# Gate logits in two halves, at steps 29 and 31, and the choice, gates and dispatch two steps later

## What is computed

```python
    x = x + _L0_conv_ref(_gn(x), ...)              # a scale per image and channel
    t = _to_tokens(x)                              # 1024 tokens of 128 per image
    t = t + _L1_attn_ref(_ln_t(t), ...)            # 8 heads of 16, softmax and a fixed decay
    t = t + _L1_ffn_ref(_ln_t(t), ...)             # 8 experts, the best 2 of each token
    x = _from_tokens(t, x)
```

```python
        logits = xf @ wg + bg
        top_vals, top_idx = jax.lax.top_k(logits, TOP_K)
        gate_w = jax.nn.softmax(top_vals, axis=-1)
```

## Time and profile before

| what | value |
|---|---|
| median of three runs | 2371.93 us |
| the profiled execution, its own time | 2371.68 us |
| its span, first to last instruction | 2369.9 us |
| PE busy, share of the span | 2076.4 us, 88% |
| DVE busy | 1897.7 us, 80% |
| ACT busy | 1460.3 us, 62% |
| POOL busy | 1019.7 us, 43% |
| largest lines of the chain that ended last | L881 22%, L893 18%, L1420 11% |
| mean granted clock of PE | 0.936 |

### The profile page before, as it was taken

How to read it: one execution, slowest core, us unless ns; L and a number is a source line. 1 busy time by engine, 2 the same in 40 slices (tenths; PEclk the granted TensorE clock), 3 DMA queues, 4 the chain that set the end, 5 groups by cost and what they waited for, 6 DMA issues and landing times.

```text
span 2369.9 us, 35246 instructions
## 1 busy us (share of the span) xinstructions
PE 2076.4 (88%) x11552; PEld 962.0 (41%) x11552; DVE 1897.7 (80%) x3669; ACT 1460.3 (62%) x2897; POOL 1019.7 (43%) x1479
## 2 busy tenths in 40 slices
PE   2699999999999999999999999999999378777743
PEld 1233343433333343334334333333433156666633
DVE  5768799999999999999999999999881366676732
ACT  1127777777777777777787777777674134344410
POOL 2101224444342444434344443433333646777764
PEclk9999999999999999999999999999995688999965
DMA  5330322323132222313222232312012277666659
GB/s 172 55 50 1 55 46 47 91 38 79 29 76 46 47 53 40 76 29 78 46 47 52 41 73 34 77 37 47 15 51 84 77 234 257 205 204 209 209 186 339
DMA packets 100990, 215.06 MB, mean 91 GB/s; under 512 B 30224, under 2 KB 50392, under 8 KB 100376
## 3 DMA queue, kind: packets, MB, share of 16 engines
q1 hardware_dynamic: 78000, 166.96, 28.7%
q0 software_dynamic: 17280, 35.95, 4.3%
q10 hardware_dynamic: 5528, 9.91, 1.2%
HBM read 104.30 MB, written 61.23 MB: 70 GB/s over the span
## 4 chain that ended last, share of the span: by engine, by line
PE 59%; DVE 16%; POOL 8%; DMA 6%; issue 5%; ACT 4%; SPq 1%; ACTq 1%; POOLq 0%; DVEq 0%
PE ps L881 22%; PE ps L893 18%; DVE row_max L1420 11%; POOL y_dram L767 7%; PE ps L860 3%; PE ps L837 2%; ACT region L1170 2%; DMA y_dram<-region 2%; DMA big<-w_dram 2%; DMA region<-y_dram 2%; DVE region L1471 2%; PE ps L845 2%; PE ps L849 2%; PE ps L912 1%; PE ps L925 1%
## 5 line engine op out<-in xcount | busy, mean ns | idle before, releaser
L1420 DVE TENSOR_REDUCE row_max<-ps 128x1 f32<-128x512 f32 x2048 | 1292.3, 680 | 133.4 <-PE ps L860 117.0
L1170 ACT ACTIVATE region<-ps 128x512 f32<-128x512 f32 x2048 | 1093.5, 602 | 377.6 <-PE ps L881 373.0
L860 PE MATMUL ps<-big 48*128 48x512 f32 x2048 | 836.8, 479 | 32.6 <-DMA big<-k_parts 14.7
L881 PE MATMUL ps<-big 50*128 50x512 f32 x2048 | 781.2, 463 | 25.9 <-ACT region L1170 15.0
L881 PEld LDWEIGHTS ps<-big 50*128 50x128 f32 x2048 | 325.9, 191 | 655.9 <-ACT region L1170 505.2
L893 PE MATMUL ps<-region 128*32 128x512 f32 x4096 | 569.7, 629 | 0.0
L860 PEld LDWEIGHTS ps<-big 48*128 48x128 f32 x2048 | 346.3, 193 | 131.8 <-DVE row_max L1420 100.1
L767 POOL DMA_INDIRECT y_dram<-region x284 | 272.0, 958 | 120.0 <-issue 82.6
L713 POOL DMA_INDIRECT xs_dram<-region,slot x256 | 249.2, 974 | 81.2 <-issue 71.8
L649 POOL TENSOR_TENSOR norm_v<-norm 128x8 f32<-128x8 f32 x32 | 6.7, 210 | 573.4 <-DVE norm L1409 573.4
L1021 PE MATMUL ps<-big 128*128 128x512 f32 x284 | 125.9, 443 | 73.2 <-DMA big<-w_dram 72.7
(11 more groups left out here) (183 smaller groups left out, 2032.1 us busy)
## 6 DMA issues: line engine op xcount, KB each, us to landing
big<-w_dram SPq DMA_DIRECT2D x71, 514.0 KB, 4.6
big<-q_parts SPq DMA_DIRECT2D x384, 64.0 KB, 2.4
big<-k_parts SPq DMA_DIRECT2D x372, 64.0 KB, 2.4
region<-xs_dram SPq DMA_DIRECT2D x71, 264.0 KB, 2.9
region<-y_dram SPq DMA_DIRECT2D x16, 1024.0 KB, 10.0
region<-in_x SPq DMA_DIRECT2D x28, 512.0 KB, 5.2
t_dram<-region SPq DMA_DIRECT2D x16, 512.0 KB, 3.4
out<-region ACTq DMA_DIRECT2D x16, 512.0 KB, 6.0
```

The lines of the kernel that those rows point to most:

```text
L860: pe.matmul(ps[:, M_BANK + half % M_BANKS, :], lane_rows(q_stack[k % 2], h, SHIFT_ROW)[:, t * P:(t + 1) * P], lane_rows(k_stack[k % 2], h, ...
L881: pe.matmul(ps[:, E_BANK + score % E_BANKS, :], lane_rows(k_stack[k % 2], h, STACK)[:, t * P:(t + 1) * P], lane_rows(q_stack[k % 2], h, ST ...
L1170: act.activation(probs[:, u % 2, step_head(k, s, i), :], ps[:, E_BANK + score % E_BANKS, :], ACT.Exp, scale=DH ** -0.5).then_inc(exp_done, 1)
L1420: dve.tensor_reduce(row_max[:, c, h * TILES + t:h * TILES + t + 1], ps[:, M_BANK + half % M_BANKS, :], AX.X, ALU.max).then_inc(max_done, 1)
```

## The change

The eight logit matmuls are cut into two halves of four tiles, at steps 29 and 31. The first half waits for the side bank, the second signals that both are there; `logits_out` moves to step 31. The first turn of the attention output moves from 31 to 33, the two projections of k from 33 and 35 to 35 and 37 (iterations 1 to 13), the seven pieces of the choice from 31 to 43 to 33 to 45, the exponential of the gap to 47, the gates to 49. The dispatch and the second values swap: dispatch from 49 to 51, values from 51 to 49.

```diff
-AT_PREP = ((1, 3), (15, 17), (23, 25), (33, 35))
+AT_PREP = ((1, 3), (15, 17), (23, 25), (35, 37))
...
-AT_LOGITS = 29
-AT_TURN_O = (31, 47, 53)
-AT_VZ = (45, 51, 59, 61)
+AT_LOGITS = (29, 31)
+AT_TURN_O = (33, 47, 53)
+AT_VZ = (45, 49, 59, 61)
...
-AT_DISPATCH = 49
+AT_DISPATCH = 51
...
-AT_GAP = 45
-AT_PICK = (31, 33, 35, 37, 39, 41, 43)
-AT_GATES = 47
+AT_GAP = 47
+AT_PICK = (33, 35, 37, 39, 41, 43, 45)
+AT_GATES = 49
...
-            def gate_logits(k):
-                pe.wait_ge(side_free, side_at["logits", k, 0])
-                for t in range(TILES):
+            def gate_logits(k, c):
+                if c == 0:
+                    pe.wait_ge(side_free, side_at["logits", k, 0])
+                for t in range(4 * c, 4 * c + 4):
...
-                mm.then_inc(side_ready, 1)
+                if c:
+                    mm.then_inc(side_ready, 1)
...
-                    if post and s == AT_LOGITS:
-                        gate_logits(it - 1)
+                    if post and s in AT_LOGITS:
+                        gate_logits(it - 1, AT_LOGITS.index(s))
...
-                    if post and s == AT_LOGITS:
+                    if post and s == AT_LOGITS[1]:
                         logits_out(it - 1)
```

More of the change, by code:

```diff
@@ L136, in side_order @@
         steps = [(AT_MAX1 if it else AT_MAX1_FIRST, "max", it, 1), (AT_TURN_O3, "turn_o", it - 1, 3), (AT_MAX0 if it >= 0 else AT_MAX0_FIRST, "max", it + 1, 0),
-                 (AT_LOGITS, "logits", it - 1, 0), (AT_DISPATCH, "dispatch", it - 1, 0)]
+                 (AT_LOGITS[0], "logits", it - 1, 0), (AT_DISPATCH, "dispatch", it - 1, 0)]
         if it == IMAGES - 1:
```

## The result

The changed kernel takes 2404.53 us, the median of 4 runs (2385.61 to 2420.08), against 2371.4 us for the kernel before: ratio 1.014, 95% interval 1.0097 to 1.0183. It is slower by about 33 us. The prediction said 2361.5 us and a range of 2348 to 2384, with a chance of 0.16 for slower: it was wrong, and in sign.

What follows compares the result with a forecast made beforehand. DVE was taken to set the pace in steps 29 to 45, PE up to step 60. From 2371.68 us, -3.4 - 5.9 - 9.1 + 4.7 + 3.5 = -10.2 gave 2361.5 us, range 2348 to 2384.

Steps and rivals of the forecast that it cites:

- the price of the late load: Load of x behind the later k projection: ACT waits at step 48, costing 4.7 us plus 3.5 for slow issues.
- the falls behind the logits: Seven clock falls to 0.50 in iterations 1 to 14 were to go with halved logits: gain 9.1 us.
- the gain in quiet iterations: Over 14 iterations, 3.4 us from halved logits and 5.9 us from the later choice.
- The three long rows of issues: SP's issues of k taking 8.75 instead of 7.58 us in three iterations: 1.17 us each, 3.5 us together.
- The absorption: Behind ACT's scaling of x, 0.5 of the 0.89 us wait was to be made up, leaving 0.39 in 12 iterations.
- The first rival: Load late by the full two steps, ACT waits 1.64 us, clock falls in six iterations: 2390.5 us; chance 0.17.
- the second rival: Clock falls stay, because they are not due to the length of the logits: 2370.6 us; chance 0.15.
- the two falls priced at 1.1 us each: Clock falls in iterations 13 and 14, which had no undisturbed neighbour of the same make; part of the 9.1 us.
- Halves: Logits in two halves end DVE's 0.24 us idle behind them in 14 iterations: gain 3.4 us.
- the last piece: Seventh piece of the choice, 0.42 us, hidden behind DVE's wait for PE at step 45: 5.9 us in 14 iterations.
- The third rival: The choice's last piece is not hidden at step 45, so its 5.9 us go: 2367.4 us; chance 0.10.
- The last image: Rival: in iteration 15 halved logits keep the clock up for half the slow stretch, 9 us more: 2352; chance 0.08.

Runs made afterwards that it cites:

- the first pair: Changed kernel without and with the load of x issued ahead of the DMAs of q and k: ratios 1.014 and 1.0011 to the kernel before.
- the third: Kernel before with only the k projection two steps later, without and with the load of x ahead of q and k: ratios 1.0098 and 0.9989.
- the early load: Changed kernel with SP's load of x issued at the start of the iteration, ahead of the DMAs of q and k: 2376.9 us, ratio 1.0011.
- the one with whole logits: Changed kernel with the eight logit matmuls back in one piece at step 29: 2407.7 us, ratio 1.0125.
- the one with k alone late: Kernel before with only the k projection moved, from steps 33 and 35 to 35 and 37: 2401.5 us, ratio 1.0098.
- the store in six: Kernel before with the store of t2, ahead of the load of x on SP, cut into six stores: 2378.1 us, ratio 1.0007.
- quarters: Changed kernel with the load of x ahead of q and k, and logits two tiles at a time at steps 28 to 31: 2374.3 us, ratio 1.001.
- a fourth of the matmuls: Changed kernel with the load of x ahead of q and k, and two logit matmuls instead of eight (different results): 2368.8 us, ratio 0.9964.
- the late choice alone: Kernel before with only choice, gap, gates and dispatch two steps later and second values at 49; logits whole, k in place: 2392.3 us, ratio 1.0065.

## Why the prediction was wrong

**Two steps failed: the price of the late load, and the falls behind the logits.** The prediction had -10.2 us and the measurement +33, 43 us apart. Some 18 to 23 of these are the late load, some 15 the falls behind the logits, which did not go, and some 4 the gain in quiet iterations. With the load's price alone put right, the sum would have been some 2379 to 2384 us, the upper end of the range; it took the second step as well to leave it.

**The price of the late load.** The sum had +8.2 us for it (4.7 and 3.5). Three pairs of kernels that differ only in when the load goes out give the price by their ratios, taken of 2372 us: 1.014 less 1.0011 is 31 us, 1.0125 less 1.0011 is 27 us, 1.0098 less 0.9989 is 26 us, each uncertain by some 11 to 16 us either way, by the intervals in the table. The profiles say the same: iterations 1 to 14 differ by 29.4 us in the first pair (1490.0 - 1460.6) and by 23.3 in the third (1481.8 - 1458.5). How much ACT waits was forecast about right; that it costs its full length, and that the clock falls more, was not:

- *The size.* The sum had 10.7 and 3.5 us of waiting, 14.2, before anything was absorbed; 15.1 were measured. That is close, and partly luck. In quiet iterations the wait was shorter than the 0.89 us, 0.65 us in iteration 4, with errors that nearly cancel: k came 2.90 us later, not 2.53, while the scaling was due 0.20 us earlier, not 0.66 (673.63 is 32.20 us behind the logits; 32.40 before). The three long rows of issues were there: SP took 8.45 us in the seventh iteration, 8.65 in the eighth and 8.28 in the tenth. What the sum did not have is that a fall behind the logits makes the wait longer. In iteration 11 the split of k begins 21.74 us behind the logits, 5.1 us later than in the quiet fourth (16.62), while ACT comes to the scaling 36.62 us behind them, only 4.4 us later (32.20). That makes 0.7 us more of wait, and iterations 5, 9, 10 and 12 are alike. The split and the scaling of iteration 11, whose logits begin at 1390.53 us:

```profile
1412.27 2.92 POOL L676 TENSOR_TENSOR k_parts<-region,k_parts 128x256 fp32r<-128x256 f32 x4 [14.66 <-ACT region L1136]
...
1428.64 1.24 ACT L1114 ACTIVATE region<-region,offset,slope 128x1024 f32<-128x1024 f32 x1 [1.49 <-DMA region<-in_x]
```

- *The absorption.* I took 0.5 us per iteration, 6.0 in twelve, as made up behind the scaling, because ACT makes up the 1.24 us of the scaling itself. The wait is not made up. The quiet iterations 1, 2, 3, 4 and 6 of the changed kernel took 0.8 to 1.0 us longer than the 102.92 of the early load, for waits of 0.65 to 0.88 us. From step 46 to 58 iteration 11 took 18.79 us before and 18.90 with the early load; in the changed kernel's iteration 3 it is 19.74, so 0.84 us more, for a wait of 0.73. The starts of ACT's exponentials, before, then early load, then changed kernel (its step 46, then 58; step 46 before is in the earlier trace rows):

```profile
1406.56 1.57 ACT L1170 ACTIVATE region<-ps 128x512 f32<-128x512 f32 x3 [0.77 <-PE ps L881]
```

```profile
1388.22 1.08 ACT L1173 ACTIVATE region<-ps 128x512 f32<-128x512 f32 x2 [1.21 <-PE ps L882]
...
1407.12 1.08 ACT L1173 ACTIVATE region<-ps 128x512 f32<-128x512 f32 x2 [0.89 <-PE ps L882]
```

```profile
565.16 0.60 ACT L1172 ACTIVATE region<-ps 128x512 f32<-128x512 f32 x1 [1.21 <-PE ps L881]
...
584.90 1.09 ACT L1172 ACTIVATE region<-ps 128x512 f32<-128x512 f32 x2 [0.89 <-PE ps L881]
```

- *The clock.* Some 12 to 16 us of the three prices are more than the waits in the table, 15.1, 15.3 and 10.6 us. The first rival had a part of this: a wait that brings PE to a stop and the clock down, deciding from about 1.5 us. The six falls at steps 48 to 51 of the changed kernel, the one with whole logits and the one with k alone late stood behind waits of 1.43 to 2.21 us, though some waits of that size passed without one; none stood behind a shorter wait, and with 10 us they came every time. But these six are the smaller part. In the three kernels, in this order, the clock was at 0.50 for 10, 17 and 3 us behind the wait, in two, three and one falls. Behind the logits of iterations 1 to 14 it was at 0.50 for 85, 96 and 72 us, in 6, 11 and 13 falls; in the same three with the early load for 55, 48 and 31 us, in 4, 6 and 7. So with the wait in the loop more falls come at the next logits, some 70 us behind it, and that no rival had. It is one profile for each kernel, and why it is so is not shown. The rival's 2390.5 us were the nearest of the numbers given, by a fall at the wait in six iterations where there were two; its chance, 0.17, was too small all the same: the forecast lay 0.6 us of waiting away from it, and the issues of k alone vary by more.

A rule of the Trainium skill (page "TensorE: Matmul & The Clock Gate", section "HAM oscillation — how this bites in real kernels") puts falls down to gaps in which PE waits. The falls behind the wait agree (PE busy 4.47 of 6.12 us, and 3.82 of 8.24); those behind the logits do not, as far as the trace can tell (3.41 of 3.41, with ends of matmuls that are modelled).

**The falls behind the logits** (-9.1 us, all to go with the halves) stayed, so the second rival was true as well. With halves and the early load there were four in iterations 4, 8, 13 and 14, each 13.65 us and some 4.4 us of time: 17.8 us. The 9.1 of before was itself too low. With the store in six, iterations 13 and 14 pass without a fall in 101.78 and 101.84 us, against 103.10 and 105.23 before, so the two falls priced at 1.1 us each cost 1.3 and 3.4, and the seven together some 11.6. The reason given, that no long stretch without 512-wide matmuls is left, was not the cause: quarters and a fourth of the matmuls have falls at the same place.

**The gain in quiet iterations** (-3.4 and -5.9 us) came in part, and for other reasons. Halves gave nothing instead of 0.24 us. The later choice gave 0.50 us from the logits to step 46 (28.02 us before, 27.52 with the early load, 1388.22 - 1360.70, where its logits begin) instead of 0.42, and lost 0.10 of it by step 58. It was put down to the last piece, hidden at step 45; that piece alone is worth 0. Together -5.6 us in 14 iterations instead of -9.3. The third rival (the last piece has no cover) does not describe this either.

**The last image** did not change: 114.7 us, 114.8 before.

So without the wait the sum over iterations 1 to 14 would have been -5.6 + 17.8 - 11.6 = +0.6 us, and the run with the early load shows 1460.6 against 1458.8, 1.8 more.

**What stays open.** What brings a fall at steps 29 to 31 in one iteration and not in the next; why its length differs between kernels (3.4 to 6.8 us behind halves at steps 28 and 29, 13.65 and once 17.07 behind halves at 29 and 31 with the late choice); why a wait at step 48 brings more falls at the logits; why the late choice alone has more and longer falls (2392.3 us) than the whole change with the early load; and why iterations 1 to 14 that are 11 us shorter leave the median where it was. Each kernel has one profile, and its runs differ by 17 to 38 us in groups of ten and more, so falls that a profile shows need not be those of the median.

## What to carry to other kernels

Before a producer is moved later, follow all that is queued behind it on the issuing engine, here a load for another image behind twelve DMAs of k: its slack, not the moved work's, decides, and it is spent first. A wait in a stretch where PE sets the pace should be priced at its full length, with what the clock takes besides in a loop that shows falls already (here some 12 to 16 us on 11 to 15 of waiting), and where the room left is about the scatter of the issue times, the case in which the wait is long should be the forecast. Then move the load along with its producer, or take it out of that queue, in the same change.

## What the hardware did that was not expected

- A store cut into three pieces of 42 and 43 partitions made the next load on the same queue land in 17.0 us instead of 5.2 (median of twelve); cut into eight pieces of 16, in 3.7.
- Falls can follow each other in step with the iterations. From iteration 9 to 13 of the changed kernel five came 109.2 us apart, in iterations of about 109 us, while in the kernel before they came in every second iteration from 2 to 8, 208.2 us apart. The changed kernel's iterations 9 to 13 in one window:

```profile
1171.70:1715.63 543.93, 532.28 (x3086) 212.81 (x3085) 487.70 (x968) 399.70 (x762) 208.95 (x348) 0.93 0.25 49
```

- A cleaner stretch did not make a faster kernel: 11.4 us less in iterations 1 to 14, and a ratio of 1.0001 [0.9971, 1.0032].
